# First attention: value products of the two key tiles in three parts over row halves and two banks, and the head transposes issued behind the scores

## The reference

```python
B, T, D, N, K, H = (4, 512, 256, 16, 8, 128); WINDOW = 128
q = rope(rms_norm(einsum('btd,ndh->btnh', x, q_kernel)))
k, v = einsum('bsd,ckdh->cbskh', x, kv_kernel)      # k also normed and roped
mask = (j <= i) & (i - j < WINDOW)
logits = where(mask, einsum('btkgh,bskh->bkgts', q * ATTN_SCALE, k), min)
probs = softmax(logits)
enc = einsum('bkgts,bskh->btkgh', probs, v)
x = x + einsum('btnh,nhd->btd', enc, out_kernel)
```

## Time and profile before

| | us |
|---|---|
| median of 3 runs | 1405.19 |
| lowest and highest | 1402.77, 1406.04 |
| profiled execution, own time | 1407.15 |
| its span, first to last instruction | 1405.4 |
| TensorE busy in the span | 1348.3 (96%) |
| VectorE busy in the span | 1059.2 (75%) |
| mean granted TensorE clock | 0.975 |

### The profile page before, as it was taken

The page is one execution under the profiler, slowest core; times in us unless marked ns, Lnnn a source line. Parts: engine busy times, 40 slices in busy tenths (PEclk is TensorE's granted clock), DMA queues, the critical chain, the costliest instruction groups (busy, mean ns, idle before and its releaser), DMA issues.

```text
span 1405.4 us, 25530 instructions
## 1 busy us (share of the span) xinstructions
PE 1348.3 (96%) x8050; PEld 1071.8 (76%) x8050; DVE 1059.2 (75%) x2468; ACT 729.2 (52%) x1899; POOL 477.2 (34%) x728
## 2 busy tenths in 40 slices
PE   5799999999999999899999999999999999999898
PEld 3588988988899889778888888888874344444487
DVE  6889999989999999667755455554658877777475
ACT  4775565556555655444432232232326676766465
POOL 5766657765776576300000000000003031331031
PEclk9999999999999999989999999999997899999899
DMA  5200000000000000055411211112253333331001
GB/s 179 83 37 1 2 1 2 2 3 1 1 1 1 1 1 1 4 156 154 142 40 61 68 40 64 62 42 93 66 173 106 107 120 121 117 120 65 0 17 44
DMA packets 45892, 80.92 MB, mean 58 GB/s; under 512 B 5608, under 2 KB 13928, under 8 KB 45484
## 3 DMA queue, kind: packets, MB, share of 16 engines
q1 hardware_dynamic: 45484, 79.35, 17.6%
q0 software_dynamic: 288, 0.10, 0.1%
HBM read 64.70 MB, written 15.87 MB: 57 GB/s over the span
## 4 chain that ended last, share of the span: by engine, by line
PE 68%; DVE 13%; issue 4%; POOL 3%; ACT 2%; DMA 0%; DVEq 0%; SPq 0%; ACTq 0%; POOLq 0%
PE ps L1416 13%; PE ps L1418 13%; PE ps L1417 13%; PE ps L1689 6%; PE ps L1728 5%; PE ps L1503 3%; PE ps L1459 3%; DVE ssum L805 2%; PE ps L1814 2%; DVE qkn L794 2%; PE ps L1837 2%; DVE yT L769 2%; PE ps L1702 1%; PE ps L1714 1%; POOL rope L534 1%
## 5 line engine op out<-in xcount | busy, mean ns | idle before, releaser
L1005 DVE TENSOR_REDUCE nm<-ps 128x1 f32<-128x512 f32 x256 | 166.3, 684 | 53.5 <-PE ps L1689 53.0
L1338 ACT ACTIVATE pT<-ps 128x512 f32<-128x512 f32 x256 | 143.2, 598 | 68.3 <-PE ps L1702 66.7
L1416 PE MATMUL ps<-xnT_lo,w1moe_hi 128*128 128x512 f32 x400 | 160.5, 401 | 0.2 <-DVE sg L919 0.2
L493 POOL TENSOR_TENSOR ln_rs<-ln_ve,minus_half 128x4 f32<-128x4 f32 x12 | 15.1, 1260 | 425.7 <-DVE ln_ve L666 425.7
L1418 PE MATMUL ps<-xnT_hi,w1moe_hi 128*128 128x512 f32 x400 | 159.3, 398 | 0.0
L1417 PE MATMUL ps<-xnT_hi,w1moe_lo 128*128 128x512 f32 x400 | 159.2, 398 | 0.0
L919 DVE TENSOR_TENSOR sg<-ps,sg 128x512 f32<-128x512 f32 x100 | 69.0, 690 | 113.9 <-ACT sg L1266 113.7
L1249 ACT ACTIVATE moe_act_hi<-sg 128x512 fp32r<-128x512 f32 x100 | 63.2, 632 | 151.3 <-DVE sg L929 147.4
L1416 PE MATMUL ps<-wqkv_lo,xnT_hi 128*128 128x512 f32 x256 | 127.2, 497 | 7.3 <-DVE wqkv_lo L718 3.1
L534 POOL TENSOR_TENSOR rope<-rope 128x384 f32<-128x384 f32 x128 | 132.6, 1036 | 0.0
L1266 ACT ACTIVATE sg<-ps 128x512 f32<-128x512 f32 x100 | 59.6, 596 | 123.3 <-PE ps L1418 123.3
(11 more groups left out here) (202 smaller groups left out, 3748.1 us busy)
## 6 DMA issues: line engine op xcount, KB each, us to landing
c_rows<-comb_rows SPq DMA_DIRECT2D x36, 256.0 KB, 3.3
copies<-qk_hi SPq DMA_DIRECT2D x32, 256.0 KB
qst<-copies SPq DMA_DIRECT2D x32, 256.0 KB, 2.6
kst<-copies SPq DMA_DIRECT2D x32, 256.0 KB, 3.0
yT<-in_w1moe SPq DMA_DIRECT2D x25, 256.0 KB, 2.6
x_res<-in_wqkv SPq DMA_DIRECT2D x8, 512.0 KB, 4.4
copies<-qk_lo SPq DMA_DIRECT2D x16, 256.0 KB
c_rows<-comb_rows SPq DMA_DIRECT2D x16, 224.0 KB, 3.1
```

Of the source, the lines that this page charges most:

```text
L1005: V.tensor_reduce(nm1[:, n % 2, t, col:col + 1], ps[:, 1 + s1_slot(p), :], AX.X, ALU.max, negate=True).then_inc(s1_max, 1)
L1338: A(pT1[:, u % 2, 2 * (m % 2) + h, c, :], ps[:, 4 + e % 2, :], ACT.Exp, scale=SCALE1).then_inc(p1_ready, 1)
L1416: MM(out, left[0], right[1], start=first, stop=False, skip_group_check=True)
```

## The change

- `quartered(m)` is true for groups that are not alone and are not the fifth or sixth of their eight. Their value products are four matmuls of 128 columns instead of two of 256: part 1 for the late queries and part 0 for the early ones over all 128 rows, then part 1 for the early queries over rows 0 to 63 and part 0 for the late ones over rows 64 to 127. The early queries are collected in bank 5, the late ones in bank 6, in the last 128 columns of each (`heads_out`). ScalarE and VectorE read them from there.
- Before them TensorE also waits for `qkT_ready` of group n - 3.
- The transposes of the heads and of the row tiles go to bank 5 (was 2), those of the probabilities to bank 2 (was 5).
- The head transposes are issued behind the scores instead of ahead of them, except in the sixth of every eight steps, and wait also for `enc_split` of this step's group where that is quartered.

```diff
+        def quartered(m):
+
+            return not alone(m) and m % GROUPS not in (4, 5)
+
+        def heads_out(m):
+
+            if not quartered(m):
+                return ps[:, 6, 0:2 * P].rearrange("p (h a f) -> p a h f", h=2, a=2)
+            return ps[:, 5:7, 3 * P:4 * P].rearrange("p a (h f) -> p a h f", h=2)
+
+        by_half = lambda e: e.rearrange("p (h a f) -> p a h f", h=2, a=2)
         weighted_tile = lambda j: -1 if j == 0 else j - 2 if j >= 2 else None
...
                 dve.wait_ge(tile_high, b * TT + t + 1)
-                V.tensor_tensor(xnT[1][:, :, at], ps[:, 2, 0:D].rearrange("p (c f) -> p c f", c=KT), xnT[0][:, :, at],
+                V.tensor_tensor(xnT[1][:, :, at], ps[:, 5, 0:D].rearrange("p (c f) -> p c f", c=KT), xnT[0][:, :, at],
                                 ALU.subtract).then_inc(tile_ready, 1)
...
                     dve.wait_ge(enc_high, k + 1)
-                    V.tensor_tensor(enc[1][:, s, :], ps[:, 6, 0:2 * P], enc[0][:, s, :], ALU.subtract
+                    V.tensor_tensor(by_half(enc[1][:, s, :]), heads_out(m), by_half(enc[0][:, s, :]), ALU.subtract
                                     ).then_inc(enc_split, 1)
...
                 act.wait_ge(tile_turned, b * TT + t + 1)
-                A(xnT[0][:, :, at], ps[:, 2, 0:D].rearrange("p (c f) -> p c f", c=KT), ACT.Copy).then_inc(tile_high, 1)
+                A(xnT[0][:, :, at], ps[:, 5, 0:D].rearrange("p (c f) -> p c f", c=KT), ACT.Copy).then_inc(tile_high, 1)
...
                         act.wait_ge(probT_parted, b * OLDER_STEPS + with_older(m - 2))
-                    A(probT[:, s], ps[:, 5, 0:2 * P].rearrange("p (h f) -> p h f", h=2), ACT.Copy).then_inc(probT_ready, 1)
+                    A(probT[:, s], ps[:, 2, 0:2 * P].rearrange("p (h f) -> p h f", h=2), ACT.Copy).then_inc(probT_ready, 1)
                 m = n - 9
...
                         act.wait_ge(heads_used, k - 1)
-                    A(enc[0][:, s, :], ps[:, 6, 0:2 * P], ACT.Copy).then_inc(enc_high, 1)
+                    A(by_half(enc[0][:, s, :]), heads_out(m), ACT.Copy).then_inc(enc_high, 1)
                 if new:
...
                     act.wait_ge(qk_turned, k + 1)
-                    A(qkT[:, m % K_RING, :, :], ps[:, 2, 0:3 * P].rearrange("p (h f) -> p h f", h=3), ACT.Copy
+                    A(qkT[:, m % K_RING, :, :], ps[:, 5, 0:3 * P].rearrange("p (h f) -> p h f", h=3), ACT.Copy
                       ).then_inc(qkT_ready, 1)
...
                 for c in range(KT):
-                    ins = T(ps[:, 2, c * P:(c + 1) * P], xn[:, i, c * P:(c + 1) * P], ident[:])
+                    ins = T(ps[:, 5, c * P:(c + 1) * P], xn[:, i, c * P:(c + 1) * P], ident[:])
                 ins.then_inc(tile_turned, 1)
...
                                  start=True, stop=True, skip_group_check=True)
+                    elif quartered(m):
+
+                        pe.wait_ge(qkT_ready, k0 + (n - 2 if new else min(n - 2, 0)))
+                        every, early, late = slice(0, P), slice(0, P // 2), slice(P // 2, P)
+                        for part, half, rows in ((1, 1, every), (0, 0, every), (1, 0, early), (0, 1, late)):
+                            queries = late if half else early
+                            ins = MM(heads_out(m)[:, half], v0[rows, (m if part else m - GROUPS) % V_RING, :],
+                                     parted[rows, r, part, :, queries], start=rows == every, stop=rows != every,
+                                     skip_group_check=True)
                     else:
...
                     ins.then_inc(projected, 1)
-                m = n - 2
-                if valid(m):
-
-                    k = k0 + m
-                    pe.wait_ge(qk_normed, k + 1)
-                    if old or m >= 1:
-                        pe.wait_ge(qkT_ready, k)
-                    if new and (following or n // GROUPS < TT - 1) and n % GROUPS == 6:
-                        pe.wait_ge(tile_ready, b * TT + n // GROUPS + 2)
-                    for h in range(3):
-                        ins = T(ps[:, 2, h * P:(h + 1) * P], qkn[:, m % 2, h * P:(h + 1) * P], ident[:])
-                    ins.then_inc(qk_turned, 1)
+                def turn_heads():
+
+                    m = n - 2
+                    if valid(m):
+
+                        k = k0 + m
+                        if valid(n - 9) and quartered(n - 9):
+                            pe.wait_ge(enc_split, k0 + n - 8)
+                        pe.wait_ge(qk_normed, k + 1)
+                        if old or m >= 1:
+                            pe.wait_ge(qkT_ready, k)
+                        if new and (following or n // GROUPS < TT - 1) and n % GROUPS == 6:
+                            pe.wait_ge(tile_ready, b * TT + n // GROUPS + 2)
+                        for h in range(3):
+                            ins = T(ps[:, 5, h * P:(h + 1) * P], qkn[:, m % 2, h * P:(h + 1) * P], ident[:])
+                        ins.then_inc(qk_turned, 1)
+
+                if n % GROUPS == 5:
+                    turn_heads()
                 m = n - 3
...
                     ins.then_inc(scored, 1)
+                if n % GROUPS != 5:
+                    turn_heads()
                 if new and (following or n // GROUPS < TT - 1) and n % GROUPS == 5:
...
                     for h in range(2):
-                        ins = T(ps[:, 5, h * P:(h + 1) * P], prob[:, m % PROB_RING, h, :], ident[:])
+                        ins = T(ps[:, 2, h * P:(h + 1) * P], prob[:, m % PROB_RING, h, :], ident[:])
                     ins.then_inc(prob_turned, 1)
```

## The result

The changed kernel takes 1425.15 us (median of 4, 1422.08 to 1427.29) against 1405.62 (4 runs, 1402.77 to 1406.54): the ratio is 1.0142, 95% interval 1.0122 to 1.0163, some 20 us slower. The profiled execution took 1427.01 us, 19.9 above that of before.

What follows compares the result with a forecast made beforehand. TensorE, busy 96% of the span, was taken to bound the kernel, VectorE following 0.1 us behind. Terms 15.1 + 2.3 - 1.5 + 1.3 - 0.5 = +16.7 us gave a forecast of 1422 us, range 1413 to 1433.

Steps and rivals of the forecast that it cites:

- The value products: First attention, 72 quartered steps: new products take 1.07 to 1.08 us against 0.87, +0.21 a step, +15.1 us in all.
- (d): Drain at the end, no projections to cover the wait for VectorE's half: +1.0, and +0.3 for the step behind.
- The copies from two banks: ScalarE's and VectorE's parts of the heads, read from two banks: no more elements, taken at nothing.
- (a): ScalarE's copy of the transposed heads, needed by the next value product: met with 0.10 us to spare, 0; if missed, +7 us.
- (b): Moved transposes wait for VectorE's half where it lags: about 0.7 in step 17, 0.1 in step 18, three batches, +2.3 us.
- (c): Step 14: the transposes' wait for the next row tile's split is covered behind the scores, -0.5 x 3 = -1.5 us.
- (e): Fill of batch 0: scores run while the transposes wait for VectorE, whose chain sets the pace; -0.5, bounds -2 and +1.
- steps 8 to 15 short of step 14 unchanged: Sign expected in the changed profile: the steps from 8 to 15, apart from a shorter step 14, keep their length.
- (1): Rival: array shape changes are free; product takes 0.67 us, VectorE sets a pace of about 4.25, 1396 us; chance 0.12.
- (2): Rival: shape changes cost only the standing still, the weight load hidden; product 0.85, no difference, 1407 us; chance 0.06.
- (3): Rival: the 64-row halves' passes do not overlap; one pair serial +0.32 a step, 1430, wholly serial 1438 us; chance 0.14.
- (4): Rival: the new wait binds every step, ScalarE's copy late by 0.1 to 0.2; +7 to +14, 1429 to 1436; chance 0.10.

## Why the prediction was right, and where it was not

Forecast 1422 us, +16.7; measured 1425.15, +19.5 (19.9 in the profiles), with an interval from 17.2 to 22.9 that leaves the +16.7 just outside. Point by point:

- **The value products**, +0.21 us a step from the earlier trace rows: +0.20 in the steps, 1.07 us as worked out, and each of its parts has an experiment: the overlap of the halves (0.22), the change of shape (0.20), the plain records (0.90 for eight). 65 of the 72 lie before the last projection, +13.1 us; seven are in the drain, which took 1.1 us more in all, these seven and the waits of (d) together. The term of 15.1 was 2.0 us too high for that.
- **The copies from two banks** at nothing: right, the means in the stage are 418 and 379 ns after, 416 and 380 before.

```profile
L787 DVE TENSOR_TENSOR enc_lo<-ps,enc_hi 128x256 fp32r<-128x256 f32 x118 | 49.3, 418 | 26.4 <-ACT enc_hi L1179 25.6
L1179 ACT ACTIVATE enc_hi<-ps 128x256 fp32r<-128x256 f32 x118 | 44.8, 379 | 0.0
```

- **(a) The copy for the next value product**: met, as said, with about 0.1 us to spare. ScalarE's copy ends at 314.73 + 0.49 = 315.22 and the next value weights load at 315.36. No step shows a wait there.

```profile
314.73 0.49 ACT L1195 ACTIVATE qkT<-ps 128x384 f32<-128x384 f32 x1 [0.56 <-PE ps L1511]
```

- **(b) VectorE's half**, +2.3 us for three batches: right in place and size. Step 17 of batch 2, 0.7 us longer, step 18 by 0.04:

```profile
378.59 0.50 PE L1427 MATMUL ps<-wqkv_lo,xnT_hi 128*128 128x512 f32 x1
...
380.08 1.05 PE L1530 MATMUL ps<-qkT 128*128 128x128 f32 x8
381.63 0.55 PE L1511 MATMUL ps<-ident,qkn 128*128 128x128 f32 x3 [0.49 <-DVE enc_lo L787]
```

```profile
381.16 0.41 DVE L787 TENSOR_TENSOR enc_lo<-ps,enc_hi 128x256 fp32r<-128x256 f32 x1
```

VectorE's half ends at 381.57, 2.98 after the projection's start, and the transposes start then. One more such step, 26 of the last batch, costs 0.37, which the prediction did not have.
- **(c) The stall of step 14** went, 0.5 us in each of three batches, as the earlier trace rows had it, with 0.1 more in step 12.
- **(d) The drain**: +1.3 forecast, +1.1 found. Its first step stands for VectorE's half as the earlier trace rows let expect:

```profile
588.21 1.03 PE L1474 MATMUL ps<-parted,v 128*128 128x128 f32 x8
589.17 1.16 PE L1530 MATMUL ps<-qkT 128*128 128x128 f32 x8
590.73 0.55 PE L1511 MATMUL ps<-ident,qkn 128*128 128x128 f32 x3 [0.41 <-DVE enc_lo L787]
```

- **(e) The fill of batch 0**: -0.5 forecast; steps 0 to 11 took 0.85 us less. That is within what the fill moves by.
- **What was missing**: 5.3 us in steps 12 and 14 to 20 of batch 0. The prediction named ScalarE's copy and exp as queued behind the moved transposes, and looked at the copy only for the next value product. In the first half of batch 0 a third instruction stands between copy and exp, the normalising, and TensorE's last item of the same step waits for it. The step that failed is that list: of who is queued behind the waiting copy it left out the one that is there in 16 steps only. The prediction's own sign, steps 8 to 15 short of step 14 unchanged, fails here: steps 12 and 15 of batch 0 are 4.63 for 3.96. The trace of before held a hint: from 36 to 110 us TensorE waits on the same pair of lines there too, in six of the seven cases ahead of step 12; from step 12 to 110 us it is once there, and eight times in the changed kernel.

```profile
PE ps L1532 <- ACT yT L1194: 5.1, 7, 1.3
```

The errors have both signs (+5.3 missing, 15.1 for 13.1, the fill 0.35 less than taken; step 26 and the steps up to the first, 0.4 and 0.6, not foreseen) and partly cancel: that the time came out only 3 us above the forecast, inside the range, is in part luck. Of the rivals, free changes of shape (1), a hidden load (2), which leaves 0.09 us for a change where the runs have 0.20, and passes that don't overlap (3) are each refuted by a run; the wait for the copy (4) by the profile alone, since taking that wait out would not leave the bank free and was not tried. The row that spoke for (1), 32-column records with no gap at 937.22, stands: the 0.20 us are shown for changes between 128 and 64 rows only. The gap that (1) gives the 128*32 records of the second attention (L1728, at columns 0, 32, 64 and 96) is some 0.1 us each way in the trace of before: on the way in from 1158.15 to the load at 1158.25; on the way out the second passes start at 1158.70, 0.45 behind the first, are through at about 1159.13 with 0.43 a pass, and the next load starts at 1159.24. That load had waited for VectorE too by the view, but the distance from load to load is the same 0.99 from 1076.70 to 1077.69, where no other engine is named. The pace of 4.25 us that (1) took for VectorE has no row; it was busy for 4.29.

## What to carry to other kernels

Halving the rows of a product paid less here than its two changes of shape cost: 0.22 us of matmul was saved and 0.40 paid, and a product with a third more columns in one shape was 8 us faster. Before splitting anything, put half-row products next to one another (apart they cost 42 us more) and see that each visit to the other shape saves more than the two changes cost, 0.4 us in these runs. When an item moves in one engine's order, list what is queued behind its copy on every other engine for each part of the program, the fill too, and who waits for each.

## What the runs showed that was not expected

The last step of batch 1, where the loop turns, took 6.2 to 7.7 us in the eight profiles against the 4.4 to 5.2 of an ordinary step, with TensorE idle for 1.6 to 1.9 us on nothing that the profile names; the kernel with the normalising ahead and the one before:

```profile
300.96 1.85 PE L1474 MATMUL ps<-parted,v 128*128 128x128 f32 x8 [1.86 <-issue]
...
303.33 0.63 PE L1428 MATMUL ps<-wqkv_hi,xnT_lo 128*128 128x512 f32 x1
303.76 0.63 PE L1429 MATMUL ps<-wqkv_hi,xnT_hi 128*128 128x512 f32 x1
```

```profile
295.19 1.13 PE L1459 MATMUL ps<-parted,v 128*128 128x256 f32 x4 [1.87 <-issue]
```

The idle time is the same, what follows is not: that step and the next took 7.70 and 5.15 us in the first of these and 6.53 and 4.40 in the second. In the first the projection matmuls behind the idle time start 0.43 us apart, where they are 0.23 apart elsewhere: the granted clock is 0.50 from 301.1 to 304.5 us, and 1.00 in the 3.5 us ahead of it and behind it. That is some 1.6 us of the two steps. The kernels with four changes of shape (324.5 to 327.9 us) and with both halves on the same rows (313.4 to 316.8) have such a stretch, at 0.50 too, at the same place; the other five have none there, though TensorE was busy up to the turn and then idle for 1.6 to 1.9 us in all eight.

So a single profile of such a kernel carries up to 2 us that can't be put down to the edit, and the granted clock of the stretch has to be read before two profiles are subtracted. Why TensorE stands at the turn, and why the clock falls behind it in three of eight profiles, stays open.
